# Scaling the keys straight out of PSUM in a chunked delta-rule layer

## The chip, the cores and the metric

The kernel runs on one core of one Trainium2 chip. The metric is the device time of one execution in microseconds (us). A core has a matrix engine (PE, its weight loads are PEld), a vector engine (DVE), a scalar engine (ACT), a general engine (POOL) and a sync engine (SP) that issues DMAs. Each takes its instructions strictly in the order of its own program, and waits at semaphores that other engines raise. Matrix products land in PSUM, in eight banks; everything else lies in SBUF.

## The reference, cut to what matters

The model is one block of four residual layers over x (4 sequences of 1024 tokens, 256 channels): latent attention, a gated recurrence ("ffn"), a chunked delta rule, and the gated recurrence again, each behind a layer norm. Only the third is touched:

```python
h = silu(sum(conv_w[:, i] * xp[:, i:i + L, :] for i in range(Kc)))
q = l2norm(h @ Wq); k = l2norm(h @ Wk)        # 4 heads of 32
v = h @ Wv                                     # 4 heads of 64
beta = sigmoid(h @ Wb)
# per head, chunk by chunk, S is the state:
kb = kc * bc[:, None]
A = tril(kb @ kc.T, -1)
U = solve_triangular(eye + A, vc * bc[:, None] - kb @ S, lower=True)
o = qc @ S + tril(qc @ kc.T) @ U
S = S + kc.T @ U
out = (o * rsqrt(mean(o * o) + eps) * norm_w * (g * sigmoid(g))) @ Wo    # g = h @ Wg
```

## The kernel before, in words

The delta layer (class `Delta`) cuts the 1024 tokens into 32 chunks of 32 tokens. A chunk holds the same 32 tokens of all 4 sequences, so it fills 128 partitions. All engines walk through the same "slots", from -5 to 51: in slot c chunk c is projected, chunk c-1 is turned and multiplied with itself (`LAG_PROD`), chunk c-14 meets its inverse (`LAG_TX`), chunk c-15 makes its output terms (`LAG_W`), and chunk c-16 updates the state (`LAG_S`). The order on every engine is the order in which the code of its method is written, slot by slot.

What the change touches, for one chunk c:

- PE, in slot c: two matmuls make q, k and beta's input, 260 columns, in the bank `qk_bank` (line 1336); two more make v and the gate, 512 columns, in `vg_bank` (line 1341). Then come the products of chunk c-1 (line 1350), from slot 15 on also the matmuls of lines 1359, 1365, 1370 and 1379, and the transposes of lines 1387 and 1396. From slot 16 on the state matmuls of lines 1323 and 1327 stand ahead of line 1336. Since `qk_bank` is one bank, line 1336 of chunk c must wait until the bank has been read for chunk c-1.
- ACT, in slot c: squares of q and k (line 1434), beta (1437), a copy of q to SBUF (1440), a copy of k to `k_raw` (1443), the gate's sigmoid (1446). The copy of k raises `q_rows`, and with it the bank is free.
- DVE, in slot c, in this order: scale k of chunk c-1 by 1/|k| and by beta/|k| (line 1509; `k_rows` is its signal), transpose (1516), in every fourth slot layer-norm statistics, from slot 16 on lines 1537 and 1542 on the output, sums of squares of chunk c (1548), in two of four slots the convolution (1557, 1563), v times beta (1571), gate (1576), masks of chunk c-1 (1584, 1590), then 1598 and 1607. From slot 9 on single steps of a triangular solve (1482, 1487) are put between these.
- POOL, in slot c: clip and power of the sums (1272, 1275), times beta (1278, signal `factors`), which line 1509 of the next slot needs. In every fourth slot the layer norm of the next tokens stands ahead of them; in two of four slots the product of line 1284 follows.

Of four slots, 3, 7, 11, ... hold the statistics and the layer norm; 0, 4, 8, 12, ... hold neither these nor a convolution and are short; 1, 2, 5, 6, ... hold a convolution.

Of the kernel before, what the change touches and what calls it, by code (L numbers as in the profile page):

```python
# [11 lines left out]
ACT = mybir.ActivationFunctionType  # L12
AXIS_X = mybir.AxisListType.X

P = 128
# [3 lines left out]
KT = C // P  # L19
BANK = 512  # L20
GROUPS = TOKENS // BANK
TPG = BANK // P
# [10 lines left out]
DH, DK, DV = 4, 32, 64  # L33
# [8 lines left out]
class Signal:  # L42
# [3 lines left out]
    def __init__(self, nc, ctx, name, by=1):  # L46
        self.handle, self.name, self.by = ctx.enter_context(nc.semaphore(name)), name, by
        self.count, self.value = 0, {}
# [1042 lines left out]
KEEP, GATES, SUMS = 16, 17, 24  # L1091
# [3 lines left out]
class Delta:  # L1095
# [4 lines left out]
    NQ, QK, HV, TAPS = 2 * DH * DK, DH * DK, DH * DV, 4  # L1100

    def __init__(self, k, x_ready, before):
        self.k, self.before = k, before
        NQ, QK, HV, TAPS = self.NQ, self.QK, self.HV, self.TAPS
        with ExitStack() as ctx:
            def sb(name, shape, dt=F32):
                return ctx.enter_context(k.nc.sbuf_tensor("d_" + name, shape, dt))

            def ring(name, n, shape):
                return [sb(f"{name}{i}", shape) for i in range(n)]  # L1110

            self.w_qkb = sb("w_qkb", [P, KT, NQ + DH])
            self.w_vg = sb("w_vg", [P, KT, 2 * HV])
            self.w_o = sb("w_o", [P, KT, C])
            self.conv = sb("conv", [P, KT, 4])
            self.norm_w = sb("norm_w", [P, KT])
            self.xg = ring("xT", 2, [P, KT, B, TAPS - 1 + P])
            self.acc = sb("conv_sum", [P, B * P])
            self.sig = sb("conv_sig", [P, B * P])
            self.hT = ring("hT", 2, [P, KT, TPG, B, CH])  # L1120
            self.sq = sb("squares", [P, NQ])
            self.ss = ring("sumsq", SUMS, [P, 2 * DH])
            self.k_raw = ring("k_raw", 2, [P, QK])
            self.factor = ring("k_factors", 2, [P, 2, DH])
            self.beta = ring("beta", 2, [P, DH])
            self.turned = ring("qT_kT_kbT", 2, [P, 3, QK])
            self.keep = ring("attnT_k_kb_v", KEEP, [P, 5, QK])
            self.qT = ring("qT_eye", KEEP, [P, 2, QK])
            self.gate = ring("gate", GATES, [P, HV])
            self.a_rows = ring("a_rows", 2, [P, DH, CH])  # L1130
            self.sys_a = sb("systems", [P, CH, CH])
            self.inv = sb("inverse", [P, CH, CH])
            self.prod = sb("products", [P, CH, CH])
            self.invT = ring("inverses", 3, [P, DH, CH])
            self.wu = ring("w_u", 2, [P, DH, CH + DV])
            self.dm = ring("q_left_decay", 2, [P, DH, 2, CH])
            self.state = ring("state", 2, [P, DH, DV])
            self.osq = sb("o_squares", [P, HV])
            self.oss = ring("o_sumsq", 2, [P, TPG, DH])
            self.on = ring("o_rows", 2, [P, TPG, HV])  # L1140
            self.oT = sb("oT", [P, KT, B, TPG, CH])
        self.ln = k.xn[0:2]
        self.x_ready = x_ready
        self.norm = k.shared_signals("ln_", "d_", "stats moments eps negmean rstd normed turned")
        self.s = k.stage_signals(
            "d_", "wo eye zeroed pad xT conv sigm hT qk_mm beta squares q_rows sums clipped k_rnorm factors q_eps "
            "k_rows rows_T qT vg_mm sgm bv gate prod_mm attnT a_rows inv_zero inv_one inv_mul inv_add tx_mm wu "
            "w_mm au_mm dm chain_mm state qs_mm o_sq o_row o_sum o_eps o_sc o_pow o_norm oT_turned oT out_mm joined",
            "w_in sys_out0 sys_out1 sys_in inv_out inv_in0 inv_in1 inv_in2")
# [158 lines left out]
    def tensor(self, e, unmet):  # L1308
        k, s, norm = self.k, self.s, self.norm
        QK, NQ, HV = self.QK, self.NQ, self.HV  # L1310
        qk_bank, vg_bank, prod_bank, tx_bank, s_bank, o_bank = k.bank[2:]
        turn_free = [self.before, self.before]
        blocks = [(h, b, slice(CH * b, CH * (b + 1))) for h in range(DH) for b in range(B)]
        for slot in range(FIRST_SLOT, LAST_SLOT):
            G, step = self.front(slot)
            Go, ostep = self.output(slot)
            c = slot - LAG_S
# [12 lines left out]
            c = slot  # L1330
            if self.chunk(c):
                cols = self.columns(c)
                for w in unmet(s["hT"](c // TPG, KT - 1), s["w_in"](4), *([s["q_rows"](c - 1)] if c else self.before)):
                    e.wait_ge(*w)
                for kt in range(KT):
                    m = e.matmul(qk_bank[:, 0:NQ + DH], cols[kt], self.w_qkb[:, kt, :], start=kt == 0, stop=kt == KT - 1)  # L1336
                m.then_inc(*s["qk_mm"].did(c))
                for w in unmet(s["gate"](c - 1) if c else None):
                    e.wait_ge(*w)
                for kt in range(KT):  # L1340
                    m = e.matmul(vg_bank[:, :], cols[kt], self.w_vg[:, kt, :], start=kt == 0, stop=kt == KT - 1)  # L1341
                m.then_inc(*s["vg_mm"].did(c))
            c = slot - LAG_PROD
# [9 lines left out]
            c = slot - LAG_W  # L1353
# [19 lines left out]
            c = slot - LAG_TX  # L1373
# [36 lines left out]
    def scalar(self, e, unmet):  # L1410
        k, s, norm = self.k, self.s, self.norm
        NQ, QK, HV, TAPS = self.NQ, self.QK, self.HV, self.TAPS
        qk_bank, vg_bank, prod_bank, tx_bank, s_bank, o_bank = k.bank[2:]
# [4 lines left out]
        for slot in range(FIRST_SLOT, LAST_SLOT):  # L1418
            G, step = self.front(slot)
            Go, ostep = self.output(slot)  # L1420
            c = slot - LAG_S
# [8 lines left out]
            c = slot  # L1430
            if self.chunk(c):
                for w in unmet(s["qk_mm"](c), s["sums"](c - 1) if c else None):
                    e.wait_ge(*w)
                e.activation(self.sq[:, :], qk_bank[:, 0:NQ], ACT.Square).then_inc(*s["squares"].did(c))
                for w in unmet(*([s["factors"](c - 2), s["bv"](c - 2)] if c >= 2 else [])):
                    e.wait_ge(*w)
                e.activation(self.beta[c % 2][:, :], qk_bank[:, NQ:NQ + DH], ACT.Sigmoid).then_inc(*s["beta"].did(c))
                for w in unmet(s["au_mm"](c - KEEP) if c >= KEEP else None):
                    e.wait_ge(*w)
                e.activation(self.keep[c % KEEP][:, 0, :], qk_bank[:, 0:QK], ACT.Copy)  # L1440
                for w in unmet(s["k_rows"](c - 2) if c >= 2 else None):
                    e.wait_ge(*w)
                e.activation(self.k_raw[c % 2][:, :], qk_bank[:, QK:NQ], ACT.Copy).then_inc(*s["q_rows"].did(c))
                for w in unmet(s["vg_mm"](c), s["o_row"](c - GATES) if c >= GATES else None):
                    e.wait_ge(*w)
                e.activation(self.gate[c % GATES][:, :], vg_bank[:, HV:2 * HV], ACT.Sigmoid).then_inc(*s["sgm"].did(c))
            c = slot - LAG_TX
# [42 lines left out]
    def vector(self, e, unmet):  # L1490
        k, s, norm, bcast, heads = self.k, self.s, self.norm, self.bcast, self.heads
        QK, NQ, HV, TAPS = self.QK, self.NQ, self.HV, self.TAPS
        qk_bank, vg_bank, prod_bank, tx_bank, s_bank, o_bank = k.bank[2:]
        solving = iter(())

        def solve(steps):
            for _ in range(steps):
                next(solving, None)

        for slot in range(FIRST_SLOT, LAST_SLOT):  # L1500
# [3 lines left out]
            c = slot - LAG_PROD  # L1504
            if self.chunk(c):
                keep = self.keep[c % KEEP]
                for w in unmet(s["factors"](c), s["q_rows"](c), s["au_mm"](c - KEEP) if c >= KEEP else None):
                    e.wait_ge(*w)
                e.tensor_tensor(keep[:, 1:3, :].rearrange("p a (h d) -> p a h d", h=DH),
                                self.k_raw[c % 2][:, :].rearrange("p (o h d) -> p o h d", o=1, h=DH).to_broadcast([P, 2, DH, DK]),  # L1510
                                self.factor[c % 2][:, :, :].rearrange("p a (h o) -> p a h o", o=1).to_broadcast([P, 2, DH, DK]),
                                ALU.mult).then_inc(*s["k_rows"].did(c))
                solve(1)
                for w in unmet(s["k_rows"](c), *([s["prod_mm"](c - 2), s["qT"](c - 2)] if c >= 2 else [])):
                    e.wait_ge(*w)
                e.transpose(self.turned[c % 2][:, :, :].rearrange("p a x -> p (a x)"), keep[:, 0:3, :].rearrange("p a x -> p (a x)")
                            ).then_inc(*s["rows_T"].did(c))
                solve(1)
# [13 lines left out]
            c = slot - LAG_S  # L1532
# [11 lines left out]
            c = slot  # L1544
# [21 lines left out]
            c = slot  # L1566
# [12 lines left out]
            c = slot - LAG_PROD  # L1579
# [14 lines left out]
            c = slot - LAG_W  # L1594
# [124 lines left out]
```

## Time and profile before

| | us |
|---|---|
| median of 3 runs (1424.62 to 1430.66) | 1424.82 |
| the profiled execution, its own time | 1424.82 |
| its span | 1423.0 |
| PE busy, x13530 | 1208.3 (85%) |
| DVE busy, x1900 | 882.7 (62%) |
| ACT busy, x1239 | 614.7 (43%) |
| POOL busy, x663 | 452.2 (32%) |

The span is the time from the first to the last instruction of the profiled execution; 1.8 us lie around it. Busy shares are means over four layers with different limits, so they say little on one of them. The delta layer's chunks 0 to 31 are projected between 846 us and about 1107 us of the span; its last slots run to about 1230 us. The profiled execution is the median run, so sums against its rows need no correction to the median.

### The profile page before, as it was taken

The page shows a single profiled execution, that of the slowest core. Times are in us where ns is not written, and L with a number is a line of the kernel's source. Part 1 is how long each engine was busy: PE and PEld are TensorE (multiplying, and loading weights), DVE is VectorE, ACT ScalarE, POOL GpSimd, SP SyncE. Part 2 cuts the span into 40 slices and gives each one's busy share as a digit, 9 for nine tenths or more (in the row PEclk, how much of TensorE's full clock was granted, in tenths as well). Part 3 has the DMA queues.
Part 4 walks back from the last instruction along what each step waited for, and adds up shares of the span by engine and source line. Part 5 has one row for each costly group of instructions (what it writes and reads, how often), then busy time and mean ns, then how long its engine had stood idle before and what let it go on. Part 6 is the DMA issues. An engine that isn't in the chain of part 4 may idle for free. (4 is left out here: it accounts for less than half of the span.)

```text
span 1423.0 us, 32391 instructions
## 1 busy us (share of the span) xinstructions
PE 1208.3 (85%) x13530; PEld 750.8 (53%) x13530; DVE 882.7 (62%) x1900; ACT 614.7 (43%) x1239; POOL 452.2 (32%) x663
## 2 busy tenths in 40 slices
PE   3779999999999999998999827557988758699992
PEld 1434444444444444436888614335666646588882
DVE  4467767676788787714443657787967462353446
ACT  1426666666666666674322223213333212242222
POOL 2420505141200000004321357554664313343204
PEclk7889999999999999998999959888999989799996
DMA  5492535354434543000000000111111100000003
GB/s 156 130 147 98 90 46 90 46 90 57 79 47 60 62 59 49 2 1 1 1 1 0 0 31 10 25 29 33 33 29 35 34 25 12 2 1 1 1 1 118
DMA packets 78754, 61.66 MB, mean 43 GB/s; under 512 B 41360, under 2 KB 65552, under 8 KB 78480
## 3 DMA queue, kind: packets, MB, share of 16 engines
q1 hardware_dynamic: 77456, 57.18, 22.4%
q10 hardware_dynamic: 1152, 2.41, 0.5%
q8 instruction: 106, 1.74, 0.5%
q14 instruction: 40, 0.33, 0.1%
HBM read 38.20 MB, written 20.97 MB: 42 GB/s over the span
## 5 line engine op out<-in xcount | busy, mean ns | idle before, releaser
L694 ACT ACTIVATE weights<-psum 128x512 f32<-128x512 f32 (+1 forms) x608 | 322.4, 585 | 159.3 <-PE psum L607 156.6
L739 DVE TENSOR_REDUCE maxima<-psum 128x1 f32<-128x512 f32 (+3 forms) x432 | 262.3, 662 | 57.4 <-PE psum L538 56.3
L607 PE MATMUL psum<-q_stack,k_stack 99*128 99x512 bf16 (+3 forms) x768 | 223.8, 328 | 1.3 <-ACT weights L694 1.1
L538 PE MATMUL psum<-k_stack,q_stack 96*128 96x512 bf16 (+3 forms) x768 | 213.1, 329 | 6.0 <-DMA k_stack<-qk_parts 4.3
L624 PE MATMUL psum<-weights,v_rows 128*17 128x512 f32 (+3 forms) x1536 | 162.0, 494 | 0.1
L510 POOL TENSOR_TENSOR residual<-residual,att_o 128x256 f32<-128x256 f32 x32 | 23.2, 725 | 364.0 <-DVE att_o L772 364.0
L900 PE MATMUL psum<-f_xT,f_weights_hi 128*128 128x512 f32 x384 | 123.4, 403 | 0.0
L739 DVE TENSOR_REDUCE negmax<-psum 128x1 f32<-128x384 f32 (+3 forms) x176 | 102.3, 635 | 27.8 <-PE psum L538 26.2
L965 ACT ACTIVATE f_gates<-psum,ffn_biases 128x512 f32<-128x512 f32 x72 | 49.7, 690 | 155.8 <-PE psum L906 155.8
L607 PEld LDWEIGHTS psum<-q_stack,k_stack 99*128 99x128 bf16 x768 | 72.5, 98 | 83.1 <-ACT weights L694 38.5
L538 PEld LDWEIGHTS psum<-k_stack,q_stack 96*128 96x128 bf16 x768 | 72.3, 99 | 57.0 <-issue 8.6
L906 PE MATMUL psum<-f_state_parts,f_weights_hi 128*128 128x512 f32 x288 | 90.4, 395 | 0.0
L603 PE MATMUL psum<-identity,mask_scores 128*128 128x128 bf16 (+2 forms) x352 | 87.1, 248 | 3.7 <-DMA q_stack<-max_parts 2.6
L534 PE MATMUL psum<-mask_scores,identity 128*128 128x128 bf16 (+2 forms) x352 | 86.7, 246 | 2.4 <-DVE a_rest L730 1.2
L603 PEld LDWEIGHTS psum<-identity,mask_scores 128*128 128x128 bf16 x352 | 34.0, 97 | 96.0 <-ACT weights L694 58.0
L1341 PE MATMUL psum<-d_w_vg,d_hT 128*128 128x512 f32 x128 | 67.6, 654 | 16.4 <-DVE d_gate L1576 16.4
L900 PEld LDWEIGHTS psum<-f_xT,f_weights_hi 128*128 128x128 f32 x384 | 71.8, 191 | 16.2
L900 PE MATMUL psum<-f_xT,f_weights_lo 128*128 128x512 f32 x192 | 76.3, 398 | 0.0
L1056 DVE COPY f_hidden<-psum 128x512 f32<-128x512 f32 x16 | 11.0, 690 | 91.3 <-PE psum L918 91.3
L906 PEld LDWEIGHTS psum<-f_state_parts,f_weights_hi 128*128 128x128 f32 x288 | 54.0, 188 | 13.3
L232 POOL TENSOR_SCALAR ln_rstd<-ln_moments 128x4 f32<-128x4 f32 x24 | 11.5, 479 | 154.0 <-DVE ln_moments L225 153.6
L1451 ACT ACTIVATE d_w_u<-psum 128x384 f32<-128x384 f32 x32 | 15.7, 490 | 101.6 <-PE psum L1379 101.6
(166 smaller groups left out, 2337.9 us busy)
## 6 DMA issues: line engine op xcount, KB each, us to landing
qk_parts<-a_parts SPq DMA_DIRECT2D x32, 384.0 KB, 3.8
q_stack<-qk_parts SPq DMA_DIRECT2D x90, 128.0 KB, 7.2
k_stack<-qk_parts SPq DMA_DIRECT2D x90, 128.0 KB, 7.8
residual<-in_x SPq DMA_DIRECT2D x8, 512.0 KB, 7.5
out_x<-residual SPq DMA_DIRECT2D x8, 512.0 KB, 3.8
ffn_weights<-in_ffn_w ACTq DMA_DIRECT2D x1, 2048.0 KB, 8.8
systems<-d_a_rows SPq DMA_DIRECT2D x32, 64.0 KB, 1.8
d_systems<-systems SPq DMA_DIRECT2D x4, 512.0 KB, 3.6
```

Source lines behind the costliest of these rows:

```text
L510: e.tensor_tensor(x, x, self.onorm[(2 * u + qc) % 2][:, :, :, :].rearrange("p i h d -> p i (h d)"), ALU.add).then_inc(*s["joined"].did(u, qc))
L534: e.matmul(out[:, 0:len(heads) * width].rearrange("p (h x) -> p h x", h=len(heads))[:, :, width - P:width], k.ident16[:, :], k.mask16[:, : ...
L538: m = e.matmul(out[:, i * width:(i + 1) * width], self.qst[st][0:self.ROWS, h, qb * P:(qb + 1) * P], self.kst[st][0:self.ROWS, h, k0:k0 + ...
L603: e.matmul(out[:, 0:len(heads) * width].rearrange("p (h x) -> p h x", h=len(heads))[:, :, 0:P], k.mask16[:, :], k.ident16[:, :].rearrange( ...
L607: m = e.matmul(out[:, j * width:(j + 1) * width], self.kst[st][0:self.ROWS + self.MAX_ROWS, h, kb * P:(kb + 1) * P], self.qst[st][0:self.R ...
L624: m = e.matmul(bank[7][32 * h:32 * h + HS + 1, off:off + width], self.v_rows[:, b * QB + kb, g * HPU + h, :], self.weights[n % 2][:, h, 0: ...
L694: e.activation(self.weights[n % 2][:, heads[0]:heads[-1] + 1, 0:width], bank[self.score_bank[n, i]][:, 0:len(heads) * width].rearrange("p ...
L739: e.tensor_reduce(to, bank[self.bank[item]][:, 0:len(heads) * width].rearrange("p (h x) -> p h x", h=len(heads)), AXIS_X, ALU.max, negate= ...
L900: m = e.matmul(bank[bk][:, :], w_hi_lo[wp][:, gate, kt, ms], x[:, v, kt, :], start=q == 0, stop=t == 0 and q == len(self.TERMS) - 1)
L906: m = e.matmul(bank[bk][:, :], w_hi_lo[wp][:, 4 + gate, kt, ms], self.state_parts[j][:, v, kt, :], start=False, stop=q == len(self.TERMS) - 1)
L965: e.activation(gs[:, gate, mt, :], next_bank()[:, :], func, bias=(k.ffn_b if t else self.bias0)[:, gate, mt:mt + 1]).then_inc(*s["gate"].d ...
L1341: m = e.matmul(vg_bank[:, :], cols[kt], self.w_vg[:, kt, :], start=kt == 0, stop=kt == KT - 1)
```

## The change

`k_raw` and the ACT copy that fills it are gone. DVE reads k in `qk_bank` itself when it scales it. The copy of q now raises `q_rows`. PE's wait ahead of the q/k projection of chunk c is now on `k_rows` of chunk c-1 (DVE) in place of `q_rows` of chunk c-1 (ACT).

```diff
-            self.k_raw = ring("k_raw", 2, [P, QK])
...
-                for w in unmet(s["hT"](c // TPG, KT - 1), s["w_in"](4), *([s["q_rows"](c - 1)] if c else self.before)):
+                for w in unmet(s["hT"](c // TPG, KT - 1), s["w_in"](4), *([s["k_rows"](c - 1)] if c else self.before)):
                     e.wait_ge(*w)
...
-                e.activation(self.keep[c % KEEP][:, 0, :], qk_bank[:, 0:QK], ACT.Copy)
-                for w in unmet(s["k_rows"](c - 2) if c >= 2 else None):
-                    e.wait_ge(*w)
-                e.activation(self.k_raw[c % 2][:, :], qk_bank[:, QK:NQ], ACT.Copy).then_inc(*s["q_rows"].did(c))
+                e.activation(self.keep[c % KEEP][:, 0, :], qk_bank[:, 0:QK], ACT.Copy).then_inc(*s["q_rows"].did(c))
...
                 e.tensor_tensor(keep[:, 1:3, :].rearrange("p a (h d) -> p a h d", h=DH),
-                                self.k_raw[c % 2][:, :].rearrange("p (o h d) -> p o h d", o=1, h=DH).to_broadcast([P, 2, DH, DK]),
+                                qk_bank[:, QK:NQ].rearrange("p (o h d) -> p o h d", o=1, h=DH).to_broadcast([P, 2, DH, DK]),
```

In PE's program nothing moves, only the wait is another. These are the rows of slots 1 and 2 before; `d_w_qkb` is the weight of the q/k projection, `d_w_vg` that of v and gate:

```order
L1336 MATMUL psum<-d_w_qkb,d_hT 128x260 [waits d_q_rows]
L1336 MATMUL psum<-d_w_qkb,d_hT 128x260
L1341 MATMUL psum<-d_w_vg,d_hT 128x512 [waits d_gate]
L1341 MATMUL psum<-d_w_vg,d_hT 128x512
L1350 MATMUL psum<-d_qT_kT_kbT 32x64 [waits d_rows_T]
L1350 MATMUL psum<-d_qT_kT_kbT 32x64 x15
```

And after (line numbers of the new file are one smaller here):

```order
L1335 MATMUL psum<-d_w_qkb,d_hT 128x260 [waits d_k_rows]
L1335 MATMUL psum<-d_w_qkb,d_hT 128x260
L1340 MATMUL psum<-d_w_vg,d_hT 128x512 [waits d_gate]
L1340 MATMUL psum<-d_w_vg,d_hT 128x512
L1349 MATMUL psum<-d_qT_kT_kbT 32x64 [waits d_rows_T]
L1349 MATMUL psum<-d_qT_kT_kbT 32x64 x15
```

`d_k_rows` is raised by DVE's first instruction of the same slot, so the projection, and all that stands behind it on PE, cannot begin before that instruction has ended.

On ACT one instruction of a slot goes. Slot 2 before:

```order
L1434 ACTIVATE d_squares<-psum 128x256 [waits d_sums,d_qk_mm]
L1437 ACTIVATE d_beta<-psum 128x4 [waits d_bv,d_factors]
L1440 ACTIVATE d_attnT_k_kb_v<-psum 128x128
L1443 ACTIVATE d_k_raw<-psum 128x128 [waits d_k_rows]
L1446 ACTIVATE d_gate<-psum 128x256 [waits d_vg_mm]
```

And after:

```order
L1433 ACTIVATE d_squares<-psum 128x256 [waits d_sums,d_qk_mm]
L1436 ACTIVATE d_beta<-psum 128x4 [waits d_bv,d_factors]
L1439 ACTIVATE d_attnT_k_kb_v<-psum 128x128
L1442 ACTIVATE d_gate<-psum 128x256 [waits d_vg_mm]
```

The copy and its wait are gone; the rest keeps its order.

## Rows read from the trace of the kernel before

**Rows 1.** Busy time by stretch (PE, PEld, DVE, ACT, POOL; clock; DMA share, GB/s)

```profile
846.00:955.00 109.00, 68.78 (x600) 38.83 (x600) 84.33 (x227) 26.45 (x91) 69.14 (x129) 0.84 0.08 19
955.00:1120.00 165.00, 141.99 (x4304) 105.96 (x4308) 122.42 (x362) 53.28 (x164) 90.02 (x160) 0.94 0.15 32
```

**Rows 2.** Groups by line, 820 to 1180 us (busy, mean ns; idle before, releaser)

```profile
L1509 DVE TENSOR_TENSOR d_attnT_k_kb_v<-d_k_raw,d_k_factors 128x256 f32<-128x256 f32 x32 | 17.0, 531 | 19.2 <-POOL d_k_factors L1278 19.2
L1576 DVE TENSOR_TENSOR d_gate<-psum,d_gate 128x256 f32<-128x256 f32 x32 | 13.2, 413 | 0.0
```

**Rows 3.** Timeline of slot 24 (start, duration, instruction, idle before)

```profile
1039.86 1.14 PE L1336 MATMUL psum<-d_w_qkb,d_hT 128*128 128x260 f32 x4
...
1041.45 0.42 DVE L1548 TENSOR_REDUCE d_sumsq<-d_squares 128x8 f32<-128x256 f32 x1 [0.29 <-ACT d_squares L1434]
...
1043.17 0.42 DVE L1571 TENSOR_TENSOR d_attnT_k_kb_v<-psum,d_beta 128x256 f32<-128x256 f32 x1 [1.30 <-ACT d_gate L1446]
```

**Rows 4.** Timeline of slot 0

```profile
848.28 2.10 PE L1336 MATMUL psum<-d_w_qkb,d_hT 128*128 128x260 f32 x4 [10.46 <-POOL d_hT L1284]
...
850.83 0.42 DVE L1548 TENSOR_REDUCE d_sumsq<-d_squares 128x8 f32<-128x256 f32 x1 [3.02 <-ACT d_squares L1434]
854.11 0.42 DVE L1571 TENSOR_TENSOR d_attnT_k_kb_v<-psum,d_beta 128x256 f32<-128x256 f32 x1 [2.86 <-ACT d_gate L1446]
```

**Rows 5.** Timeline, end of slot 1 and start of slot 2, POOL and DVE

```profile
859.79 1.27 POOL L1284 TENSOR_TENSOR d_hT<-d_conv_sum,d_conv_sig 128x512 f32<-128x512 f32 x1 [0.37 <-ACT d_conv_sig L1465]
...
859.82 0.28 DVE L1590 TENSOR_TENSOR d_a_rows<-psum,mask_strict 128x128 f32<-128x128 f32 x1
860.02 1.32 DVE L1509 TENSOR_TENSOR d_attnT_k_kb_v<-d_k_raw,d_k_factors 128x256 f32<-128x256 f32 x1
...
861.87 0.38 DVE L1548 TENSOR_REDUCE d_sumsq<-d_squares 128x8 f32<-128x256 f32 x1
```

**Rows 6.** Timeline of DVE, slot 4

```profile
875.62 0.43 DVE L1509 TENSOR_TENSOR d_attnT_k_kb_v<-d_k_raw,d_k_factors 128x256 f32<-128x256 f32 x1 [4.78 <-POOL d_k_factors L1278]
...
876.88 0.41 DVE L1571 TENSOR_TENSOR d_attnT_k_kb_v<-psum,d_beta 128x256 f32<-128x256 f32 x1
...
877.74 0.28 DVE L1590 TENSOR_TENSOR d_a_rows<-psum,mask_strict 128x128 f32<-128x128 f32 x1
878.76 0.43 DVE L1509 TENSOR_TENSOR d_attnT_k_kb_v<-d_k_raw,d_k_factors 128x256 f32<-128x256 f32 x1 [0.75 <-POOL d_k_factors L1278]
```

**Rows 7.** Timeline of DVE, slots 8 and 9

```profile
901.12 0.42 DVE L1509 TENSOR_TENSOR d_attnT_k_kb_v<-d_k_raw,d_k_factors 128x256 f32<-128x256 f32 x1 [4.78 <-POOL d_k_factors L1278]
...
903.56 0.28 DVE L1590 TENSOR_TENSOR d_a_rows<-psum,mask_strict 128x128 f32<-128x128 f32 x1
905.07 0.42 DVE L1509 TENSOR_TENSOR d_attnT_k_kb_v<-d_k_raw,d_k_factors 128x256 f32<-128x256 f32 x1 [1.22 <-POOL d_k_factors L1278]
...
908.93 0.19 DVE L1482 TENSOR_TENSOR d_products<-d_inverse,d_systems 128x31 f32<-128x31 f32 x1 [1.13 <-DMA d_systems<-systems]
```

**Rows 8.** Timeline of DVE, slot 10

```profile
914.79 0.41 DVE L1509 TENSOR_TENSOR d_attnT_k_kb_v<-d_k_raw,d_k_factors 128x256 f32<-128x256 f32 x1
...
916.03 0.40 DVE L1548 TENSOR_REDUCE d_sumsq<-d_squares 128x8 f32<-128x256 f32 x1
```

**Rows 9.** Timeline of DVE, slot 12

```profile
935.04 0.42 DVE L1509 TENSOR_TENSOR d_attnT_k_kb_v<-d_k_raw,d_k_factors 128x256 f32<-128x256 f32 x1 [1.53 <-POOL d_k_factors L1278]
...
937.15 0.41 DVE L1571 TENSOR_TENSOR d_attnT_k_kb_v<-psum,d_beta 128x256 f32<-128x256 f32 x1
```

**Rows 10.** Busy time in short stretches (columns as in rows 1)

```profile
902.00:906.00 4.00, 3.79 (x43) 3.43 (x44) 2.50 (x8) 1.20 (x2) 3.43 (x9) 0.50 0.11 16
936.00:942.00 6.00, 5.66 (x46) 4.59 (x47) 5.86 (x19) 1.98 (x6) 2.28 (x5) 0.50 0.09 14
```

**Rows 11.** Timeline of slot 16, PE and DVE

```profile
964.16 1.14 PE L1336 MATMUL psum<-d_w_qkb,d_hT 128*128 128x260 f32 x4
964.92 0.43 DVE L1509 TENSOR_TENSOR d_attnT_k_kb_v<-d_k_raw,d_k_factors 128x256 f32<-128x256 f32 x1 [2.19 <-POOL d_k_factors L1278]
```

## The prediction

> **What bounds the kernel now.** I read the busy time by stretch first, then the groups by line within the delta layer, then the waits, and last the timeline slot by slot. The change touches slots 0 to 32 of one layer, some 265 us of 1423; the three other layers stay as they are. In the first 109 us of it (slots 0 to 13) DVE is busy 84 us and POOL 69, PE 69; in the next 165 us PE is busy 142 and DVE 122 [rows 1]. In both DVE sets the pace of a slot more than PE does: its first instruction of a slot, line 1509, waits in all 19.2 us for POOL's factors and is otherwise followed at once by the next [rows 2]. ACT is idle three quarters of the first stretch [rows 1], so the copy that goes costs nothing today. What matters is how far ahead of DVE the q/k projection now runs. In slot 4 DVE starts line 1509 at 875.62 and v times beta already at 876.88, without a wait [rows 6]: squares and gate of chunk 4 lay ready, since PE had projected the chunk in the slot before. That lead is what the new wait forbids.
>
> **What the change adds: a loop through PE and ACT in each slot.** PE may start the projection of chunk c only when line 1509 of slot c has ended. Counted from the start S of that instruction: it takes 0.42, and PE starts some 0.05 later. From PE's start to DVE's sums of squares (line 1548) slot 24 shows 1041.45 - 1039.86 = 1.59, and to v times beta (line 1571) 1043.17 - 1039.86 = 3.31; DVE waited in both places, so these are the bare lengths of the loop at the full TensorE clock, where the projection took 1.14 [rows 3]. In slot 0 the projection took 2.10, which is the half clock, and the two distances are 2.55 and 5.83 [rows 4]. So sums can start no earlier than S+2.06 (full) or S+3.02 (half), v times beta no earlier than S+3.78 or S+6.30. Line 1341 (v and gate) stands behind the waiting projection on PE, the products of line 1350 behind that. DVE pays where it stood at sums or at v times beta sooner than that, unless a later wait of the slot takes the loss back. Slot by slot:
>
> - Slots 1 to 3: sums of slot 2 came 0.53 after line 1509's end [rows 5]; now it is 1.59 + 0.05 = 1.64 after, so +1.1; slot 1 pays +1.0. Both get 0.9 back, see below. Slot 3 has its statistics as cover. Net +0.3.
> - Slot 4 lasted 878.76 - 875.62 = 3.14. Now v times beta starts at S+3.78, from there to the end of line 1590 it is 877.74 + 0.28 - 876.88 = 1.14 [rows 6], so the slot lasts 4.92 (full, +1.8) or 7.44 (half, +4.3).
> - Slots 5 to 7: slot 5 waits for its projection today too, slot 6 pays 1.1, both get 0.9 back: -1.2 (full) or +1.3 (half).
> - Slot 8 lasted 905.07 - 901.12 = 3.95 [rows 7]: +1.0 or +3.5.
> - Slot 9: the first solve step (line 1482) waits for a DMA round trip that starts with line 1590 of slot 8; 908.93 - 903.84 = 5.09. Line 1509 of slot 9 stood 1.23 after that line's end, for POOL; in the longer slot 8 it follows at once, so of the round trip 5.0 in place of 908.93 - 905.07 = 3.86 now fall in slot 9 [rows 7]: +1.15.
> - Slot 10: sums at S + 1.24 [rows 8], now 2.06 or 3.02: +0.8 or +1.8; v times beta has the convolution ahead of it and pays nothing. Slot 13 likewise: +0.7 or +1.7.
> - Slot 11: statistics cover it, and slot 12 begins with 1.53 of waiting for POOL [rows 9]: 0 or +1.1.
> - Slot 12: v times beta at S + 2.11 [rows 9]: +1.7 or +4.2, and nothing later in the slot waits.
> - Slots 14 and 15: 15's projection is held by the first inverse's DMA, and DVE waits 2.19 for POOL after it [rows 11]: 0 or +1.1.
> - Slot 16: the projection, which now stands behind the state matmuls, started at 964.16; line 1509 ends at 965.35 [rows 11]: +1.2. In slots 17 to 31 DVE reaches line 1509 before PE reaches the projection, or a wait for POOL like the 2.19 of slot 15 gives the loss back. The same subtraction is above zero and lasting in three: slots 19, 22 and 27, with 0.6, 0.8 and 0.8, together +2.3 (in 27 the projection would be 2.8 late, but DVE is busy with the solve and PE catches up to within 0.8).
>
> **What it takes away.** The copy of k, 32 times on ACT: 0, since ACT waits. The operand of line 1509 that lay in SBUF: of 32 instances four took 1.32 in place of 0.42, all four beside POOL's line 1284, as at 860.02; line 1590 began 0.03 us after the same POOL instruction with one PSUM operand and took its usual 0.28 [rows 5]. With k in PSUM I take all four at 0.42, -3.6 together, already in the sums of slots 1 to 3 and 5 to 7. If the release failed it would be +3.6.
>
> **PSUM as operand of line 1509.** The trace before shows no such read of k. The nearest row is line 1576, the same shape with one PSUM operand: 413 ns, against 531 on average and 419 in the undisturbed instances of line 1509 [rows 2]; so I take 0, bounds -0.2 and +0.2 us for all 32. The Trainium skill ("VectorE: DVE Perf Modes", the section on the TRN2 errata) gives a PSUM source 120 cycles of fixed cost and an SBUF source 58; by it 32 reads would cost some 2.1 us more, an estimate by that page, and the sum below would be 1445.2. The rows of this case do not bear it out for an op with two tensors.
>
> **Sum.** All at the full clock: 0.3 + 1.8 - 1.2 + 1.0 + 1.15 + 0.8 + 0 + 1.7 + 0.7 + 0 + 1.2 + 2.3 = +9.8. All of slots 4 to 15 at the half clock: 0.3 + 4.3 + 1.3 + 3.5 + 1.15 + 1.8 + 1.1 + 4.2 + 1.7 + 1.1 + 1.2 + 2.3 = +24.0. Which of the two holds where: before, PE ran at a granted clock of 0.50, the half level, in slots 8 and 12 [rows 10], each after a slot in which it had run out of work while DVE waited for POOL; the change, which holds PE back in each slot, makes such idle time longer. So slots 8 and 12 at half (+3.5, +4.2), slot 4, which begins after the same wait of 4.78 as slot 8 [rows 6, 7], a little better than half (+3.3), slots 5 to 7 full, and in slots 10, 11, 13 and 14 to 15, where PE will do its work of a slot in one burst and then idle, the middle: +1.3, +0.5, +1.2, +0.5. That gives 0.3 + 3.3 - 1.2 + 3.5 + 1.15 + 1.3 + 0.5 + 4.2 + 1.2 + 0.5 + 1.2 + 2.3 = +18.3. The slots after 32 and the second recurrence move by the same amount and neither add nor absorb. The profiled execution took 1424.82 in all, the median of the runs; 1424.8 + 18.3 = 1443.1 us.
>
> **Rivals.**
>
> 1. The clock stays up. One burst per slot in place of two might keep the clock as it was or better. Then +9.8, 1434.6 us. For it: slots 1, 2, 5 and 6 are short enough. Against: the two rows at half clock [rows 10]. The Trainium skill ("TensorE: Matmul & The Clock Gate", Part 1) has the clock fall after an idle stretch; by that the result would lie towards +24.0, an estimate from rows that the page does not enter.
> 2. The cover holds. DVE's stalls are taken back everywhere by waits for POOL, and only slots 4, 8 and 12 lose at the full clock, 4.5 less 3.6 of the release, plus slot 16: about +2, 1427 us. Against it: POOL's factors wait for sums, so outside the layer-norm slots that wait moves with the stall.
> 3. Not slower: the release of line 1509 decides. It is worth 3.6 us, and it wins alone if the loop's result is there when DVE needs it, that is if sums stand 2.06 or more behind S in nearly every slot. Then 1421.2 us. Against it: 1.24 in slot 10 and 0.53 after the end in slot 2 [rows 5, 8].
> 4. The loop rules the late slots too. If each of slots 16 to 31 pays slot 16's 1.2, 15 x 1.2 = 18 come on top, less the 2.3 counted: 1424.8 + 18.3 + 16 = 1459 us. For it: PE is the busier engine there [rows 1] and all it does for the older chunks stands behind the projection. Against: in most of these slots line 1509 ends before the state matmuls do.
>
> **How the numbers follow.** Forecast 0.60 (its own range 1437 to 1449), clock stays up 0.20, late slots too 0.07, cover holds 0.08, not slower 0.05. A measurement of this kernel can tell about 0.5%, 7.1 us, from no change. Forecast, full clock and rival 4 are above it, with a little of rival 2: slower 0.89. Within 0.5% lie most of rivals 2 and 3: 0.09. Faster by more would need twice the release: 0.02. The range that leaves out 2 in 10 runs from a little below the full-clock sum, 1431, to a little above the half-clock sum, 1450.
>
> **What would show it.** In the profile after: line 1509's successor (line 1505 of the new file) 32 times at about 0.42, none at 1.3. PE idle ahead of the q/k projection, released by that line, in most of slots 1 to 14. DVE's waits for squares at sums and for the gate at v times beta grow by some 15 us in all, while its waits for POOL ahead of line 1505 shrink a little. Slots 4 and 8 last 6 to 8 us each. It would be wrong if DVE's waits do not grow, if a PSUM operand makes line 1505 slower, or if slots after 16 lengthen by more than 4 us in sum.

## The result and the profile after

| | before | after |
|---|---|---|
| median of 6 runs, us | 1426.61 (1424.62 to 1430.66) | 1452.16 (1448.99 to 1454.23) |
| ratio | | 1.0173, 95% interval 1.0152 to 1.0193 |
| profiled execution, span | 1423.0 | 1450.8 |

The change makes the kernel 1.73% slower, 24.7 us on 1426.6. (The two medians lie 25.6 us apart, the two profiled executions 27.8.) The direction is the forecast's. The time lies above the forecast's own range (1437 to 1449) and 2 us above the upper end of the wider one (1431 to 1450).

The busy time by stretch after, with the columns of [rows 1]. The stretches cover the same slots as there (DVE has the same 227 and 362 instructions in them), so the first is 16.5 us longer, the second 9.7:

```profile
846.00:971.50 125.50, 74.69 (x632) 41.40 (x632) 81.92 (x227) 24.42 (x76) 66.72 (x129) 0.78 0.08 17
971.50:1146.20 174.70, 142.99 (x4252) 105.78 (x4248) 123.05 (x362) 50.15 (x146) 87.65 (x160) 0.92 0.14 29
```

DVE was busy 77% of the first stretch and now is 65%. The granted clock fell from 0.84 to 0.78 and from 0.94 to 0.92. The groups by line that answer to [rows 2], line 1505 being the old 1509, with PE's projection:

```profile
L1505 DVE TENSOR_TENSOR d_attnT_k_kb_v<-psum,d_k_factors 128x256 f32<-128x256 f32 x32 | 13.3, 416 | 9.1 <-POOL d_k_factors L1277 9.1
L1572 DVE TENSOR_TENSOR d_gate<-psum,d_gate 128x256 f32<-128x256 f32 x32 | 13.2, 414 | 0.0
L1335 PE MATMUL psum<-d_w_qkb,d_hT 128*128 128x260 f32 x128 | 48.0, 510 | 68.3 <-DVE d_attnT_k_kb_v L1505 57.8 <-POOL d_hT L1283 10.5
```

Line 1505 takes 416 ns in the mean, 531 before. PE stands idle 57.8 us ahead of the projection for it, a wait that did not exist. What DVE waits for in the layer (in all, times, longest):

```profile
DVE d_attnT_k_kb_v L1567 <- ACT d_gate L1442: 29.3, 18, 3.0
DVE d_sumsq L1544 <- ACT d_squares L1433: 22.1, 23, 3.0
```

Before, the same two were 10.5 us and 9.4 us. Slot 2 shows the read and the loop, as [rows 5] did:

```profile
861.70 0.41 DVE L1505 TENSOR_TENSOR d_attnT_k_kb_v<-psum,d_k_factors 128x256 f32<-128x256 f32 x1
862.14 0.58 DVE L1512 STREAM_TRANSPOSE d_qT_kT_kbT<-d_attnT_k_kb_v 128x384 f32<-128x384 f32 x1
863.76 0.42 DVE L1544 TENSOR_REDUCE d_sumsq<-d_squares 128x8 f32<-128x256 f32 x1 [1.04 <-ACT d_squares L1433]
```

```profile
861.46 1.27 POOL L1283 TENSOR_TENSOR d_hT<-d_conv_sum,d_conv_sig 128x512 f32<-128x512 f32 x1 [0.37 <-ACT d_conv_sig L1461]
```

Line 1505 runs beside POOL's product and takes 0.41, not 1.32. Sums start 2.06 behind its start, the bare loop at the full clock. (2.06 and 3.02 are what the prediction worked out for the shortest way from line 1505 over PE and ACT to the sums, at the full and at the half clock.) Slot 8, which answers to [rows 7], shows the same loop with PE mostly at the half level:

```profile
904.42 0.42 DVE L1505 TENSOR_TENSOR d_attnT_k_kb_v<-psum,d_k_factors 128x256 f32<-128x256 f32 x1 [3.80 <-POOL d_k_factors L1277]
...
907.51 0.42 DVE L1544 TENSOR_REDUCE d_sumsq<-d_squares 128x8 f32<-128x256 f32 x1 [2.06 <-ACT d_squares L1433]
910.10 0.42 DVE L1567 TENSOR_TENSOR d_attnT_k_kb_v<-psum,d_beta 128x256 f32<-128x256 f32 x1 [2.16 <-ACT d_gate L1442]
...
911.16 0.41 DVE L1505 TENSOR_TENSOR d_attnT_k_kb_v<-psum,d_k_factors 128x256 f32<-128x256 f32 x1
```

It lasts 6.74 (3.95 before), of which DVE waits 4.2. What was not foreseen stands in slot 27; DVE, then PE:

```profile
1094.83 0.42 DVE L1505 TENSOR_TENSOR d_attnT_k_kb_v<-psum,d_k_factors 128x256 f32<-128x256 f32 x1
...
1100.84 0.42 DVE L1567 TENSOR_TENSOR d_attnT_k_kb_v<-psum,d_beta 128x256 f32<-128x256 f32 x1 [2.24 <-ACT d_gate L1442]
```

```profile
1095.30 2.10 PE L1335 MATMUL psum<-d_w_qkb,d_hT 128*128 128x260 f32 x4 [2.73 <-DVE d_attnT_k_kb_v L1505]
1097.19 3.19 PE L1340 MATMUL psum<-d_w_vg,d_hT 128*128 128x512 f32 x4
```

PE idled 2.73, and then the projection took 2.10 and v and gate 3.19: half clock, in a slot that was priced at the full one.

**How the slots are compared.** The starts of the 32 instances of line 1509 (1505) are laid side by side, each counted from the kernel's first one; instance c begins slot c+1. How much later an instance comes than before is what the slots up to there have cost. In the change that is 14.8 us at instance 15 and 25.6 at instance 31 (the last). The other 2.2 of the 27.8 us between the spans lie ahead of the layer's chunks (0.7) and behind them (1.5). These figures are of one execution each, and that one is not always a typical one: it was the slowest of ten for late only (1444.77, median 1439.22) and the slowest of twelve for two banks (1430.48, median 1425.33), and the fastest of four for busy early, busy late and busy both. Where the two disagree, the ratio of the timed runs counts.

### The profile page after: what moved, and what is told of

The parts are those of the page before. It is cut to its first block and busy times, and to the rows that moved or that the text cites. A ratio compares the mean times of both kernels' runs of the same rounds, so it can differ in the third digit from the quotient of the medians.

```text
span 1450.8 us, 32359 instructions
## 1 busy us (share of the span) xinstructions
PE 1218.1 (84%) x13530; PEld 755.3 (52%) x13530; DVE 880.1 (61%) x1900; ACT 610.2 (42%) x1207; POOL 447.5 (31%) x663
## 5 line engine op out<-in xcount | busy, mean ns | idle before, releaser
L739 DVE TENSOR_REDUCE negmax<-psum 128x1 f32<-128x384 f32 (+3 forms) x176 | 102.3, 634 | 27.8 <-PE psum L538 26.2
L1335 PE MATMUL psum<-d_w_qkb,d_hT 128*128 128x260 f32 x128 | 48.0, 510 | 68.3 <-DVE d_attnT_k_kb_v L1505 57.8
L1340 PE MATMUL psum<-d_w_vg,d_hT 128*128 128x512 f32 x128 | 75.7, 724 | 0.0
L1335 PEld LDWEIGHTS psum<-d_w_qkb,d_hT 128*128 128x128 f32 x128 | 27.6, 239 | 77.0 <-DVE d_attnT_k_kb_v L1505 42.7
```

Of the source, the lines that this page charges most:

```text
L739: e.tensor_reduce(to, bank[self.bank[item]][:, 0:len(heads) * width].rearrange("p (h x) -> p h x", h=len(heads)), AXIS_X, ALU.max, negate= ...
```

## The experiments

The last two columns are those of the comparison just described.

| run | ratio to before, 95% interval | at instance 15 | at instance 31 |
|---|---|---|---|
| the change | 1.0173 (1.0152 to 1.0193) | 14.8 | 25.6 |
| wait only | 1.0201 (1.0171 to 1.0231) | 22.1 | 30.6 |
| early only | 1.0083 (1.0055 to 1.0110) | 15.6 | 16.9 |
| late only | 1.0052 (1.0034 to 1.0070) | 0.3 | 10.8 |
| copy kept | 1.0133 (1.0092 to 1.0174) | 14.7 | 22.6 |
| busy early | 1.0122 (1.0101 to 1.0143) | 10.6 | 16.4 |
| busy late | 1.0150 (1.0125 to 1.0175) | 14.9 | 20.5 |
| busy both | 1.0110 (1.0095 to 1.0126) | 12.7 | 15.3 |
| late rest | one run | 0.1 | 10.5 |
| old first | 1.0172 (1.0142 to 1.0203) | 15.8 | 25.2 |
| before again | one run | 0.0 | 0.8 |
| before, busy late | 0.9994 (0.9976 to 1.0013) | 0.1 | 0.0 |
| two banks | 0.9982 (0.9969 to 0.9995) | -4.1 | -0.3 |

**Wait only.** The kernel before with the new wait and nothing else:

```diff
-  *([s["q_rows"](c - 1)] if c else self.before)
+  *([s["k_rows"](c - 1)] if c else self.before)
```

> The kernel before, with PE's wait ahead of the q/k projection moved to k_rows of the chunk before; the copy of k on ACT stays and DVE reads the copy. Theory A (the moved wait is the whole cost, the read itself is free): as slow as the change, plus the 3.6 us of line 1509 beside POOL that are not released: 1424.8 + 27.8 + 3.6 = 1454 to 1458 us. Rival B (the read of PSUM or the missing copy costs a good part, the wait only part): 1433 to 1445 us.

Measured 1461.0 on a chip whose before was 1430.6, ratio 1.0201: in trace terms 30.6 against the change's 25.6. Theory A: its 1454 to 1458 is a ratio of 1.021 to 1.023, which the interval reaches, and rival B's 1.006 to 1.014 is far below. The moved wait alone costs all of it, and by the traces the read of PSUM gives 5.0 us back (by the timed runs the two kernels' intervals overlap). In slots 1 to 9 it gives back more than the 3.6 counted: at instance 8 this kernel is 11.8 late, the change 5.4. Rows of DVE's slots 2 and 3 here:

```profile
861.38 1.31 DVE L1509 TENSOR_TENSOR d_attnT_k_kb_v<-d_k_raw,d_k_factors 128x256 f32<-128x256 f32 x1
865.30 0.42 DVE L1548 TENSOR_REDUCE d_sumsq<-d_squares 128x8 f32<-128x256 f32 x1 [1.99 <-ACT d_squares L1434]
869.76 1.04 DVE L1509 TENSOR_TENSOR d_attnT_k_kb_v<-d_k_raw,d_k_factors 128x256 f32<-128x256 f32 x1
```

Sums stand 3.92 behind the start: 1.31 for the line itself and a loop at the half clock. Once the line is in the loop, its stall beside POOL delays PE too.

**Early only and late only.** k is read from PSUM up to chunk 14, or from chunk 15 on; the rest is the kernel before.

```diff
+def DIRECT(c):
+    return c <= 14        # late only: c >= 15
...
-  *([s["q_rows"](c - 1)] if c else self.before)
+  *([s["k_rows" if DIRECT(c - 1) else "q_rows"](c - 1)] if c else self.before)
...
+  (qk_bank[:, QK:NQ] if DIRECT(c) else self.k_raw[c % 2][:, :])
```

> The change for chunks 0 to 14 only, the kernel before from chunk 15 on. Theory A with the late slots as a loss of their own: 1424.8 + 14.8 (what the traces differ by at the start of slot 16, the start of the layer taken off) = 1439 to 1442 us. Rival C (the late loss follows from the early one, through clock or phase): 1446 us or more.

> The kernel before for chunks 0 to 14, the change from chunk 15 on. Theory A: 1424.8 + 10 to 13 = 1435 to 1438 us. The prediction on record had 3.5 here: 1428 us. Rival C: 1426 to 1430 us.

Early only 1.0083, late only 1.0052; 1.0135 together, where the change has 1.0173. In the traces the parts add: 15.6 and 10.8 - 0.3 = 10.5, against 14.8 and 10.8. But the trace of late only is of its slowest execution. By the ten timed runs the late half alone costs 7.4 us (4.9 to 10.0), which is less than theory A's 10 to 13, touches the upper edge of rival C's 1 to 5 and is more than the 3.5 on record. Early only lies below rival C's 1446 us, which would be 1.015 or more; C falls. So there is a late loss without the early one, larger than was forecast; its size is 10.5 in the trace and nearer 7 in the timed runs, and why the two halves fall 5 us short of the whole in these stays open.

**Copy kept.** The change, with ACT's copy of k put back though nobody reads it.

```diff
-  e.activation(self.keep[c % KEEP][:, 0, :], qk_bank[:, 0:QK], ACT.Copy).then_inc(*s["q_rows"].did(c))
+  e.activation(self.keep[c % KEEP][:, 0, :], qk_bank[:, 0:QK], ACT.Copy)
+  e.activation(self.k_raw[c % 2][:, :], qk_bank[:, QK:NQ], ACT.Copy).then_inc(*s["q_rows"].did(c))
```

> The changed kernel with ACT's copy of k to SBUF put back ahead of q_rows, though DVE still reads PSUM and nobody reads the copy. Theory A (the copy was free before and stays free): 0.26 us later q_rows, which DVE does not wait for; 1450 to 1454 us as the change. Rival D (ACT is now inside the loop, so the 0.3 us copy counts in each of 32 slots, in the way of the gate's sigmoid): up to +9, 1456 to 1461 us.

Ratio 1.0133, with an interval that ends at the change's ratio; rival D's 1456 to 1461 us would be 1.022 or more and falls. Theory A's 1450 to 1454 would be 1.018 to 1.021, so this kernel came out below that as well. In the traces it is 14.7 against 14.8 at instance 15 and 19.4 against 19.9 at instance 24. The copy costs nothing, as the prediction said. That this kernel later comes out 3 us ahead is not explained by the edit; it may be no more than the spread of the late half between executions.

**Busy early, busy late, busy both.** The change, with small matmuls that nobody reads on PE: behind the products in slots 3, 7 and 9 to 13 (early), or behind a wait for the gate at the end of slots 17 to 19 and 25 to 27 (late).

```diff
+EXTRA = {3: 24, 7: 24, 9: 32, 10: 34, 11: 30, 12: 26, 13: 26}
...
+  for kt in range(EXTRA.get(slot, 0)):
+      e.matmul(tx_bank[:, 0:BANK // 4], k.ident[:, :], k.ident[:, :], start=True, stop=True)
```

```diff
+LATE = {17: 14, 18: 14, 19: 8, 25: 14, 26: 20, 27: 8}
...
+  if slot in LATE:
+      for w in unmet(s["gate"](slot)):
+          e.wait_ge(*w)
+      for _ in range(LATE[slot]):
+          e.matmul(vg_bank[:, 0:P], k.ident[:, :], k.ident[:, :], start=True, stop=True)
```

> The changed kernel with 24 to 34 small matmuls more on PE behind the products in slots 3, 7, 9, 10, 11, 12 and 13, into a bank that nobody reads there, so that PE idles less ahead of the next q/k projection. Theory A2 (of the early loss some 7 us are the half clock in slots 4, 8 and 10 to 14, brought by idle time): the slots 4 to 14 run at full clock and the time falls by 4 to 7 us against the change, ratio to before about 1.013, line 1505 of slot 14 comes some 5 us earlier. Rival E (the clock is of no account, or the extra matmuls run at half clock themselves and stand in the way): equal to the change or up to 5 us above it, ratio 1.017 to 1.021.

> The changed kernel with 8 to 20 small matmuls more on PE at the end of slots 17, 18, 19, 25, 26 and 27, behind a wait for the gate, where PE would idle until DVE has finished line 1594. Theory A2 (slots 20 and 27 pay the half clock): slot 27 gives back some 2 us and slot 20 some 1 us, in all 2 to 4 us below the change, ratio to before about 1.015. Rival F (the late loss is PE's own queue being late, at any clock): no change within 1 us.

> The changed kernel with the extra matmuls of both earlier runs: slots 3, 7, 9 to 13 and 17, 18, 19, 25, 26, 27. Theory A2: the two gains add; ratio to before 1.009 to 1.012, line 1505 of slot 32 some 13 to 15 us later than before in place of 25.6. Rival E (each gain was an accident of its execution): 1.015 or more.

More work on PE makes the kernel faster: clearly so with busy early and busy both, while the interval of busy late overlaps the change's. Busy early brings 4.2 us by instance 15 and 1.0122 in place of 1.0173; busy late leaves the early half as it was (14.9) and cuts the late half from 10.8 to 5.6; both together leave 15.3 of the 25.6 and 1.0110, with 2.6 for the late half. In the timed runs the gains are 7.3, 3.3 and 9.0 us, a sum within their intervals; in the traces they overlap (9.2, 5.1 and 10.3): the late half is 5.8 with busy early alone, in which nothing late was edited, so where the half-clock stretches fall depends on what came before.

Three stretches of the change follow, the end of slot 18 with the start of 19, then slot 20 and slot 27 from end to end; below them the same of busy late, and of the kernel before (columns of [rows 1]):

```profile
1011.00:1018.00 7.00, 5.69 (x71) 4.03 (x72) 6.86 (x24) 1.39 (x5) 0.93 (x3) 0.51 0.13 21
1024.28:1033.57 9.29, 8.61 (x223) 6.33 (x227) 6.90 (x25) 2.48 (x7) 5.56 (x12) 0.82 0.06 11
1094.83:1107.17 12.34, 10.62 (x240) 7.33 (x240) 9.48 (x30) 2.26 (x7) 2.20 (x5) 0.80 0.08 14
```

```profile
1011.00:1018.00 7.00, 6.42 (x117) 4.78 (x119) 6.86 (x24) 1.61 (x6) 0.29 (x2) 1.00 0.13 21
1024.71:1032.28 7.57, 6.99 (x218) 5.36 (x222) 6.79 (x24) 2.45 (x7) 4.78 (x13) 1.00 0.10 17
1091.74:1101.86 10.12, 9.65 (x232) 7.83 (x236) 9.41 (x30) 1.88 (x6) 2.67 (x5) 1.00 0.10 17
```

```profile
994.00:1001.00 7.00, 6.58 (x76) 4.24 (x76) 6.86 (x24) 1.55 (x6) 1.25 (x3) 0.56 0.13 21
1006.63:1013.50 6.87, 6.83 (x239) 5.10 (x238) 6.73 (x25) 3.25 (x10) 4.15 (x13) 1.00 0.08 14
1073.12:1082.39 9.27, 8.15 (x241) 6.22 (x240) 9.13 (x29) 2.43 (x8) 2.30 (x5) 1.00 0.11 19
```

With the idle time filled the granted clock is 1.00 where it was 0.51. In the first stretch the kernel before stood at the half level too (0.56); there the change added little (slots 18 and 19 cost 0.4 together). Slots 20 and 27 ran at 1.00 before, at 0.82 and 0.80 in the change, and again at 1.00 in busy late. Slot 27 in busy late, DVE and PE:

```profile
1095.52 0.42 DVE L1573 TENSOR_TENSOR d_attnT_k_kb_v<-psum,d_beta 128x256 f32<-128x256 f32 x1 [0.27 <-ACT d_gate L1448]
```

```profile
1092.21 1.14 PE L1336 MATMUL psum<-d_w_qkb,d_hT 128*128 128x260 f32 x4 [0.53 <-DVE d_attnT_k_kb_v L1511]
```

The projection takes 1.14 in place of 2.10, DVE's wait for the gate 0.27 in place of 2.24; slot 27 costs 0.85 over before, not 3.07, and slot 20 costs 0.7, not 2.4. The prediction had 0.8 for slot 27 at the full clock. The traces of all the kernels with the moved wait in slot 27 fall into two groups: where its projection took 2.10 (the change, wait only, late only, copy kept, busy early) it cost 2.5 to 3.1, and where it took 1.14 or 1.15 (busy late, busy both, old first) 0.4 to 0.85. In old first no matmul was added, which speaks for the clock and against the extra work itself as the cause.

**Before, busy late.** The control: the same late matmuls in the kernel before.

> A control: the kernel before with the extra matmuls of the late slots 17, 18, 19, 25, 26 and 27, as they stood in the changed kernel. Theory A2 (they pay only because the change has put the projection, at whatever clock it runs, on DVE's path): equal to before within 0.3%, line 1509's last instance within 1.5 us. Rival L (they speed up any kernel there, since the state chain also runs at half clock): 2 to 5 us faster than before, and then the gain of the run with them says little on the change.

0.9994, 0.9976 to 1.0013, last instance 0.0. The extra work raised the clock here as well: in slots 18 and 19 before had 0.74 and 0.82, this kernel 1.00. Where PE keeps its lead that buys nothing; rival L falls.

**Late rest.** The change only for chunks 16 and up and not for the slots in which the prediction had a late loss.

```diff
+def DIRECT(c):
+    return c >= 16 and c + 1 not in (19, 22, 27)
```

> The kernel before, with the change only in those late slots in which the prediction counted no loss: chunks 16 and up, without the slots 19, 22 and 27 (and 16). The prediction on record: line 1509's last instance comes 0 us later than before. Theory G (a wait for POOL on DVE gives back DVE's loss, but not the delay of PE's queue, which returns in the next slot): 4 to 7 us later. Rival H (the late loss sits in slots 16, 19, 22 and 27, only larger than counted, through the clock): 0 to 2 us later.

Its busy time in two short stretches (columns of [rows 1]):

```profile
997.00:1004.00 7.00, 6.54 (x92) 4.36 (x96) 6.86 (x24) 1.57 (x6) 1.21 (x3) 0.60 0.13 21
1010.00:1017.00 7.00, 6.77 (x88) 3.88 (x91) 3.80 (x13) 1.00 (x4) 3.60 (x11) 0.56 0.01 2
```

10.5 us in this one execution, more than either theory: the slots that were counted as free cost what the whole late half does. The first of the two stretches was no better before (0.56, above). The second lies in slot 20, which had 1.00 before: its projection took 2.07 in place of 1.14, and it cost 4.1. So it is no matter of four slots: where the half clock falls on DVE's path moves with the edit. The figure is beyond the 4 to 7 of theory G.

**Old first.** In slots 16 and up PE does lines 1358 and 1364 of the older chunk ahead of the projection.

```diff
   c = slot - LAG_W
+  if slot >= 16 and self.chunk(c):
+      ...                    # w_mm and the s_bank group, moved up
   c = slot
   if self.chunk(c):          # q/k projection
```

> The changed kernel, but from slot 16 on PE does the two groups of matmuls of chunk c-15 that need nothing from DVE in this slot (lines 1358 and 1364) ahead of the q/k projection, not behind it, so they fill the wait for line 1505. Theory G (late, the loss is work of the older chunks queued behind the waiting projection): 2 to 5 us below the change, ratio to before 1.014 to 1.016, slots 20, 22 and 27 shorter. Rival K (late, the loss is the way of chunk c itself: projection, squares, gate): equal or up to 1 us per slot above, since the projection now starts 1.1 us later where PE was the late one.

1.0172 and 25.2: no gain. Theory G, that the late loss is old work which this order would move out of the way, falls; rival K's "equal" holds. All of PE's work between two projections is still there in this order, so the run says nothing against a loss from PE's queue as a whole.

**Before again.** A second profile of the kernel before.

> The kernel before, profiled a second time. Theory I (the late half of the layer varies from execution to execution, and the profiled execution on which the prediction rested was one of the quicker): the last instance of line 1509 comes 1 to 4 us later after the first than in the first profile, with the difference in slots 20 to 26. Rival J (the kernel before repeats itself to 0.3 us there, so everything found late is the change): equal slots.

Instances repeat within 0.1 us up to 16 and within 1.1 after, 0.8 at the last. That is between theory I's 1 to 4 and rival J's 0.3; the late loss is no accident of the first profile.

**Two banks.** k read from PSUM for chunks 0 to 13, the odd ones projected into the bank that stands empty until slot 14, so PE waits for `k_rows` of c-2.

```diff
+def qk(k, c):
+    return k.bank[5] if DIRECT(c) and c % 2 else k.bank[2]
+def bank_read(s, c):
+    if c >= 15:
+        return [s["q_rows"](c - 1)]
+    if c == 14:
+        return [s["k_rows"](12)]
+    return [s["k_rows"](c - 2)] if c >= 2 else []
```

> DVE reads k out of PSUM for chunks 0 to 13 only, and their odd ones are projected into the bank that stands empty until slot 14, so PE waits for k_rows of the chunk before the last; from chunk 14 on the kernel before. Theory A (the loss is PE's lost lead, the read itself is free and releases line 1509 beside POOL): no loss, and the four instances of 1.3 us are gone: 3 to 4 us below before, ratio 0.997 to 0.998. Rival B (reading PSUM costs by itself): above before.

Line 1527 here is the old 1509. In slot 2 it and POOL's product run at the same time, DVE's row first:

```profile
860.95 0.42 DVE L1527 TENSOR_TENSOR d_attnT_k_kb_v<-psum,d_k_factors 128x256 f32<-128x256 f32 x1
```

```profile
860.72 1.27 POOL L1300 TENSOR_TENSOR d_hT<-d_conv_sum,d_conv_sig 128x512 f32<-128x512 f32 x1 [0.37 <-ACT d_conv_sig L1483]
```

Ratio 0.9982, 0.9969 to 0.9995: a little faster than before, and so than both kernels. The read from PSUM with PE's lead kept is 4.0 us ahead at instance 9 and stays so to 15. Behind that, in code that is the kernel before's, 3.8 us were lost again in the profiled execution; the twelve timed runs keep 2.6 us. That execution was the slowest of the twelve. Part of it is the clock again: the projection of slot 20 took 1.87 there, 1.14 before, and the slot 0.8 longer. What eats the rest was not found.

## Why the prediction was wrong in its size

- **What bounds, and the loop.** Right. The bare lengths of 2.06 and 3.02 to sums came out as worked: 2.06 in slot 2, 3.09 in slot 8, where the gap ahead of the projection was 0.15 and not 0.05. PE waited for the line in 21 slots.
- **The slots 1 to 15.** Right: +14.75 forecast, +14.8 found. By parts, forecast and found: slots 1 to 3 0.3 and 0.3; 4 3.3 and 3.5; 5 to 7 -1.2 and -1.2; 8 3.5 and 2.8; 9 1.15 and 1.4; 10 1.3 and 1.8; 11 0.5 and 0.3; 12 4.2 and 4.0; 13 1.2 and 0.7; 14 and 15 0.5 and 1.2. The single terms miss by up to 0.7 us either way, so the match of the sum to 0.05 is in part luck; that of the pattern is not.
- **Slots 16 to 31: the step that failed.** Forecast 3.5, found 10.8. Slot 16 alone was right (1.2, found 1.3). Slots 19, 22 and 27 were put at 2.3 and cost 5.7, all others at 0 and cost 3.8. Most of it is two slots: 20, put at 0, cost 2.4, and 27, put at 0.8, cost 3.1. The prediction asked "which of the two holds where" only for slots 4 to 15 and took the full clock for all that follows, because PE is busier there. But slots 17 to 19 and 25 to 27 carry the solve on DVE, they last up to 15 us, and PE runs dry in them. The kernel before had its projections of slots 18, 19 and 26 at 2.10 already, the half clock, and there DVE waited for it by 0.7 us at the most; the prediction did not look there. The moved wait adds idle time ahead of the projection (1.48 in slot 20, 2.73 in slot 27), and the half clock reaches slots 20 and 27, now on DVE's path. Slots 20 and 27 in busy late show it, and the late half then costs 5.6 in busy late and 2.6 in busy both, against the forecast's 3.5 at the full clock. Two things stay open: what the late half costs in a typical execution (10.8 in the profiled one, 7.8 in copy kept, nearer 7 in the timed runs of late only), and what the other slots' rest is made of. The prediction had named "slots after 16 lengthen by more than 4 us in sum" as a sign of being wrong; slots 17 to 31 lengthened by 9.5.
- **"A wait for POOL gives the loss back."** It does in slots 21 and 29, by 1.5 and 0.8, but slots 22 and 30 then cost 2.3 and 1.4. This is PE's lateness, which a wait on DVE does not shorten. PE's projections of slots 21 and 22, after and then before:

```profile
1034.04 1.15 PE L1335 MATMUL psum<-d_w_qkb,d_hT 128*128 128x260 f32 x4
1042.62 1.14 PE L1335 MATMUL psum<-d_w_qkb,d_hT 128*128 128x260 f32 x4
```

```profile
1013.25 1.14 PE L1336 MATMUL psum<-d_w_qkb,d_hT 128*128 128x260 f32 x4
1021.82 1.14 PE L1336 MATMUL psum<-d_w_qkb,d_hT 128*128 128x260 f32 x4
```

They lie 8.6 apart in both: PE's own work sets that distance. The projection of slot 21 now stands 0.47 behind DVE's line 1505, before it stood 0.26 ahead of it, and these 0.73 are what slots 21 and 22 cost together. The prediction's 0.8 for slot 22 is right for the pair. Slots 29 and 30, put at 0, cost 0.6 together in the same way. So the mechanism was missed, but it is worth little here: the half clock in slots 20 and 27 is the larger part.
- **What it takes away.** The copy: 0, shown. The release of line 1509: 3.6 was right where PE keeps its lead (4.0 in two banks) and too small in the loop (wait only lost 6.4 more than the change by instance 8).
- **PSUM as operand.** Taken as 0: 416 ns against 419 before. The 2.1 us that the Trainium skill's cycle table would add ("VectorE: DVE Perf Modes", section on the TRN2 errata) did not appear; the measurement decides.
- **The rivals.** "The clock stays up" was wrong the other way. Its counter, the rule of the Trainium skill on idle time ("TensorE: Matmul & The Clock Gate", Part 1), agrees with 0.51 turning to 1.00 in the busy runs. "The late slots too" named the right place with another mechanism: slots 23 and 24 cost nothing. "Cover" (1427) and "not slower" (1421) fell with the result.
- **The range.** The half-clock sum, +24.0, took 3.5 for the slots from 16 on, at the full clock. With the 10.8 found in place of it, it would have stood at 1424.8 + 31.3 = 1456.

DVE's two waits at sums and at v times beta grew by 31.5 us, not by some 15, while that for POOL fell by 10.1, from 19.2 to 9.1: a third of the growth took the place of an old wait.

## What to carry to other kernels

A copy out of PSUM can be worth its time because it frees the bank: before it is removed, ask which engine frees the bank then, and how far ahead the producer ran. If the answer is the engine that sets the pace, each step now contains the whole way through producer and helper, unless a second bank keeps the lead. Price that way at both levels of TensorE's clock in every stretch where the new wait can leave PE idle, the busy-looking ones too.

## What the runs showed of the hardware that was not expected

- Useless matmuls made the changed kernel faster, 1.0173 to 1.0110, and left the kernel before as it was, 0.9994: the granted clock rose in both, from 0.51 to 1.00 at the start of slot 19 in the one and from 0.74 to 1.00 in slot 18 in the other. Only where the projection stood on DVE's path was that worth time.
- A DVE instruction with two SBUF operands took 1.3 us in place of 0.42 beside POOL's product of 128x512; with one operand in PSUM 32 of 32 took 0.41 to 0.43, the four of the same places beside it among them.
